# Layer B's context kept in HBM as f32 and shaped in layer B; affine parts and the variance's eps on VectorE

## What is computed

```python
x = x + tanh(g_xattn[0]) * L0_xattn(ctx, layernorm(x), mask, ...)   # 8 heads of 64
x = x + tanh(g_ffn[0])   * L0_ffn(layernorm(x), ...)                # 8 experts, top 2
x = x + tanh(g_xattn[1]) * L1_xattn(ctx, layernorm(x), mask, ...)   # 16 heads of 64
x = x + tanh(g_ffn[1])   * L1_ffn(layernorm(x), ...)                # quantised, depthwise conv
# in both attentions
ctx_n = (ctx - mean) * rsqrt(var + 1e-5) * gamma + beta             # gamma, beta per layer
lat_n = layernorm(latents) * gamma_lat + beta_lat
kv    = concat(ctx_n, lat_n)         # 375 + 112 = 487 keys
```

## Time and profile before

| what | us |
|---|---|
| median of 3 executions | 1544.24 |
| their range | 1537.44 to 1548.83 |
| profiled execution: span from its first to its last instruction | 1538.1 |
| PE, DVE, ACT, POOL busy in it | 1278.3, 1053.8, 979.1, 1107.9 |

### The profile page before, as it was taken

One profiled execution on the slowest core, in us unless ns is written; L12 is line 12 of the kernel. 1 busy time (PEld: TensorE's weight loads), 2 busy tenths in 40 slices (PEclk: granted clock), 3 DMA queues, 4 the chain that ended last, 5 costly groups with the idle time before them and its releaser, 6 DMA issues.

```text
span 1538.1 us, 45142 instructions
## 1 busy us (share of the span) xinstructions
PE 1278.3 (83%) x16918; PEld 994.2 (65%) x16918; DVE 1053.8 (69%) x2830; ACT 979.1 (64%) x2319; POOL 1107.9 (72%) x1359
## 2 busy tenths in 40 slices
PE   0778787679878989878999999899999999998852
PEld 0556565557667866656887887667676676766642
DVE  4768788977556656665666666777777777877634
ACT  2778787456455666554656566678777777777631
POOL 4768788687557755466777776788878888787653
PEclk9989999879999989989999999999999999999965
DMA  9599997486999954368999997344555444555310
GB/s 314 134 193 235 246 239 174 83 221 188 218 233 252 233 95 97 73 159 171 247 258 231 269 247 181 79 97 98 105 91 94 90 105 94 106 82 91 79 32 6
DMA packets 438329, 239.96 MB, mean 156 GB/s; under 512 B 388848, under 2 KB 420320, under 8 KB 429024
## 3 DMA queue, kind: packets, MB, share of 16 engines
q1 hardware_dynamic: 408216, 178.51, 55.7%
q10 hardware_dynamic: 26824, 51.22, 10.6%
q0 software_dynamic: 3072, 7.34, 1.6%
HBM read 107.78 MB, written 35.50 MB: 93 GB/s over the span
## 4 chain that ended last, share of the span: by engine, by line
PE 39%; ACT 13%; DVE 12%; POOL 11%; issue 9%; DMA 9%; DVEq 3%; SPq 2%; ACTq 1%; POOLq 0%
PE bank_ring L1088 9%; PE bank_ring L1126 6%; PE bank_ring L1074 5%; PE bank_out L1107 5%; DVE scores L1340 4%; DMA expert_up<-experts_up 4%; ACT scores L849 4%; PE bank_x L1187 3%; POOL probs L654 3%; PE bank_scores L1048 3%; ACT probs L856 3%; PE bank_x L1140 3%; DMA probs_turned<-probs 3%; ACT values L876 2%; DMA context<-in_ctx 2%
## 5 line engine op out<-in xcount | busy, mean ns | idle before, releaser
L654 POOL TENSOR_TENSOR probs<-scores,probs 112x487 f16<-112x487 f32 x384 | 425.0, 1123 | 234.2 <-ACT probs L856 229.1
L849 ACT ACTIVATE scores<-scores,score_min 112x487 f32<-112x487 f32 x384 | 265.8, 693 | 121.0 <-DVE score_min L1340 118.2
L1357 DVE SCALAR_TENSOR_TENSOR values<-bank_ring,values 128x512 f16<-128x512 f32 x192 | 132.4, 689 | 216.4 <-ACT values L876 216.3
L1340 DVE CUSTOM_DVE_ANT_0 scores<-bank_scores,mask 112x487 f32<-112x487 f32 x384 | 238.1, 657 | 2.9 <-PE bank_scores L1048 2.9
L856 ACT ACTIVATE probs<-scores 112x487 f16<-112x487 f32 x384 | 214.2, 604 | 24.4 <-DMA probs_turned<-probs 9.0
L1088 PE MATMUL bank_ring<-weights,kv_B 128*128 128x128 f16 x3072 | 198.3, 223 | 1.2 <-DVE keys L1352 1.2
L876 ACT ACTIVATE values<-bank_ring 128x512 f16<-128x512 f32 x192 | 112.9, 588 | 128.9 <-PE bank_out L1107 125.2
L1088 PEld LDWEIGHTS bank_ring<-weights,kv_B 128*128 128x128 f16 x3072 | 187.2, 100 | 10.5 <-DVE keys L1352 2.0
L1107 PE MATMUL bank_out<-values,probs_turned 128*128 128x64 f16 x4608 | 171.9, 195 | 17.7 <-issue 11.4
L1074 PE MATMUL bank_ring<-kv_B,weights 128*128 128x488 f16 x768 | 181.0, 372 | 0.0
L1107 PEld LDWEIGHTS bank_out<-values,probs_turned 128*128 128x128 f16 x4608 | 160.1, 100 | 21.4 <-issue 14.0
(11 more groups left out here) (230 smaller groups left out, 2470.9 us busy)
## 6 DMA issues: line engine op xcount, KB each, us to landing
expert_up<-experts_up SPq DMA_DIRECT2D x43, 1024.0 KB, 5.5
expert_down<-experts_down SPq DMA_DIRECT2D x43, 512.0 KB, 6.6
raw_weights<-in_weights ACTq DMA_DIRECT2D x8, 1536.0 KB, 10.7
experts_up<-expert_up ACTq DMA_DIRECT2D x8, 1024.0 KB, 4.4
raw_weights<-in_weights ACTq DMA_DIRECT2D x6, 1024.0 KB, 8.0
probs_turned<-probs SPq DMA_TRANSPOSE x384
context_turned_B<-kv_B ACTq DMA_DIRECT2D x16, 375.0 KB, 8.7
kv_B<-context_turned_B ACTq DMA_DIRECT2D x16, 375.0 KB, 3.7
```

The lines of the kernel that those rows point to most:

```text
L654: pool.tensor_tensor(PR[:, u % 4, 1, 0:KEYS], S[:, u % 4, 0:KEYS], PR[:, u % 4, 0, 0:KEYS], ALU.subtract).then_inc(probs_split, 1)
L849: act_e.activation(S[:, u % 4, 0:KEYS], S[:, u % 4, 0:KEYS], ACT.Exp, bias=rmin[:, u % 4:u % 4 + 1], scale=-1.0, accum_out=rsum[:, g % 2, ...
L1340: dve.tensor_tensor_reduce(out=S[:, u % 4, 0:KEYS], in0=bS[u % 2][0:TOK, 0:KEYS], in1=mask[:, m, 0:KEYS], scale=1.0, scalar=3.0e38, op0=AL ...
L1357: dve.scalar_tensor_tensor(vN[:, j % 2, 1].rearrange("p t d -> p (t d)"), bank("v", j)[:], 1 / WSCALE, vN[:, j % 2, 0].rearrange("p t d -> ...
```

## The change

The context of layer B is no longer finished in layer A. What goes to HBM is `rawT` itself (f32, normalised and turned, 128 rows of 3000 bytes a sequence) in place of hi and lo (also 3000 bytes a row, but in four pieces of 750 bytes). In layer B it comes back into `rawT`, DVE multiplies by gamma and adds beta in place (`shape_context`), ACT rounds it with one copy, POOL subtracts. For layer A, DVE writes the shaped f32 into `ctxA`, which lies in the second buffer of `kv[1]`, unused until layer B. The latents' affine parts are made by DVE straight from PSUM, four instructions in layer A and two in layer B in place of one copy. DVE adds the variance's eps, so that POOL's `rstd` is the power alone. `f_round` is folded into `f_scale` (add and subtract in one instruction). The mask's shaping is a function of its own behind `split_latents`, and waits for `ctx_lo` as well.

```diff
+def shape_step(n):
+    return start_b(n) - (6 if n == 0 else 8)
...
-        kv_dram = dram("context_turned_B", (NSEQ, 128, KB, 2, CTX), F16)
+        ctx_dram = dram("context_normed", (NSEQ, 128, KB, CTX), F32)
...
+        ctxA = kv[1][:, 1].rearrange("p k a c -> p (k a c)").bitcast(F32)[:, 0:KB * CTX]\
+            .rearrange("p (k c) -> p k c", k=KB)
...
             def rstd(stage, n, cols):
-                after(pool.tensor_tensor(r[:, 0:cols], m[:, 0:cols, 1], growth[:, 0:cols], ALU.mult))
-                after(pool.tensor_tensor(r[:, 0:cols], r[:, 0:cols], bias[:, 0:cols], ALU.add))
                 pool.tensor_tensor(r[:, 0:cols], r[:, 0:cols], minus_half[:, 0:cols], ALU.pow)\
                     .then_inc(rstd_ready[stage], 1)
...
-            def split_context(n, kb, layer):
-                pool.wait_ge(x1_drained, X1_AT[("p_turn", n, kb)])
-                after(pool.tensor_scalar(aff[:, 0:CTX], rawT[:, kb], ...))
-                pool.wait_ge(ctx_hi[layer], 2 * n + kb + 1)
-                pool.tensor_tensor(kv[layer][:, n % 2, kb, 1, TOK:KEYS], aff[:, 0:CTX], ...)
+            def split_context(layer, n):
+                src = ctxA if layer == 0 else rawT
+                pool.wait_ge(ctx_shaped[layer], KB * (n + 1))
+                pool.wait_ge(ctx_hi[layer], n + 1)
+                for kb in range(KB):
+                    last = pool.tensor_tensor(kv[layer][:, n % 2, kb, 1, TOK:KEYS], src[:, kb], ...)
+                last.then_inc(ctx_lo[layer], 1)
...
-                after(pool.tensor_scalar(h, h, ROUND, None, ALU.add))
-            def f_round(n):
-                pool.tensor_scalar(q2T[:, m], hacts[n % 2][:, m], ROUND, None, ALU.subtract)...
+                pool.tensor_scalar(q2T[:, 4 * j:4 * j + 4], h, ROUND, ROUND, ALU.add, ALU.subtract)\
+                    .then_inc(q2_ready, 1)
...
                 if (j + 4) % 4 == 0 and 0 < (j + 4) // 4 < NSEQ:
-                    split_context((j + 4) // 4, 1, 0)
+                    split_context(0, (j + 4) // 4)
+                for n in range(NSEQ):
+                    if j == shape_step(n) + 1:
+                        split_context(1, n)
...
             def spill_context(n):
-                act_e.wait_ge(ctx_lo[1], 2 * n + 2)
-                act_e.dma_start(kv_dram[n], kv[1][:, n % 2, :, :, TOK:KEYS]).then_inc(spilled[n % 2], 16)
+                act_e.wait_ge(x1_drained, X1_AT[("p_turn", n, 1)])
+                act_e.dma_start(ctx_dram[n], rawT[:]).then_inc(spilled, 16)
...
-                if (j + 2) % 4 == 0 and 0 <= (j + 2) // 4 < NSEQ:
-                    spill_context((j + 2) // 4)
+                if (j + 5) % 4 == 0 and 0 <= (j + 5) // 4 < NSEQ:
+                    spill_context((j + 5) // 4)
...
-                    if j == start_b(n) - (6 if n < 2 else 7):
+                    if j == shape_step(n) - 2:
                         reload_context(n)
...
+            def round_context(layer, n):
...
+                act_e.wait_ge(ctx_shaped[layer], KB * (n + 1))
+                act_e.activation(kv[layer][:, n % 2, :, 0, TOK:KEYS], ctxA if layer == 0 else rawT[:], ACT.Copy)\
+                    .then_inc(ctx_hi[layer], 1)
...
             def round_latents(n):
-                        last = act_e.activation(dst[:, kb, 0], latT[:, kb], ACT.Identity, scale=scale, bias=shift)
+                act_e.activation(latq[:, n % 2, :, 0], latT[:, 0], ACT.Copy)
+                act_e.activation(kv[0][:, n % 2, :, 0, 0:TOK], latT[:, 1], ACT.Copy).then_inc(lat_hi[0], 1)
...
+            def shape_context(n):
...
+                dve.wait_ge(ctx_back, 16 * (n + 1))
+                for kb in range(KB):
+                    scale, shift = latent_vec(8 + V_GAMMA, kb)
+                    dve.tensor_scalar(rawT[:, kb], rawT[:, kb], scale, shift, ALU.mult, ALU.add)\
+                        .then_inc(ctx_shaped[1], 1)
...
                 if name == "p_turn":
                     if n:
-                        dve.wait_ge(ctx_lo[0], 2 * (n - 1) + kb + 1)
-                        dve.wait_ge(ctx_lo[1], 2 * (n - 1) + kb + 1)
+                        dve.wait_ge(spilled, 16 * n)
+                        dve.wait_ge(ctx_lo[0], n)
                     dve.tensor_copy(rawT[:, kb], bX1[:, 0:CTX]).then_inc(x1_drained, 1)
+                    dve.drain()
+                    dve.tensor_scalar(ctxA[:, kb], rawT[:, kb], scale, shift, ALU.mult, ALU.add)\
+                        .then_inc(ctx_shaped[0], 1)
                 elif name in ("p_lat", "b_lat"):
-                    dve.tensor_copy(latT[:], bX1[:, 0:KB * TOK]...).then_inc(x1_drained, 1)
+                    for i, c in enumerate((8 + V_GLAT,) if layer else (V_GLAT, V_GATED)):
+                        for kb in range(KB):
+                            last = dve.tensor_scalar(latT[:, i, kb], bX1[:, TOK * kb:TOK * kb + TOK], scale, shift,
+                                                     ALU.mult, ALU.add)
```

150 lines of the change are left out of this document (60 added, 90 removed).

## The result

The changed kernel is slower: 1564.38 us median (4 runs, 1559.36 to 1570.24) against 1546.53 for the kernel before (4 runs, 1537.44 to 1549.43), a ratio of 1.0126 [1.0085, 1.0166]. The forecast was 1524.

The account below looks back on a forecast made before the run. No engine is full; waits in each engine's order of work count, PE's largest being for POOL's mask (29.5 us). Terms -10, 0, -7, -2, +1.5, +2, -4.4 sum to -20: span 1518, median 1524; 8-in-10 range 1503 to 1552.

Parts of the forecast that it names:

- Loop 62 to 263: Layer A's seven sequences beside the expert weights: POOL's and ScalarE's relief less VectorE's added work, -10 us.
- I take half: Layer A loop: of 3.0 us a sequence if all terms lay in series, 1.5 counted, times seven sequences.
- absorbed: Rival: relieved engines did not set layer A's step, VectorE fills the gap; -5 us, 1539; chance 0.22.
- 263 to 340: Routing stretch, VectorE fullest: its +5 us for two sequences is given back by work leaving POOL's queue; 0.
- 340 to 575: First expert tiles: POOL's shorter queue lets probabilities and expert loads go earlier; -7 us (0 to -16).
- The spill: Context's DMA to HBM: fewer runs, so its issue holds ScalarE less; -2 us (0 to -7).
- a late spill: Rival: spills behind 3 MB of weights land too late for VectorE's next copy; +9 on the forecast, 1533; chance 0.08.
- Prologue: Start: first spill stands behind the third context's load and the next copy follows at once; +1.5 us.
- The end: Last steps, POOL on the chain: f_round goes and two rstd are shorter; -4.4 us (-2.5 to -5).
- Layer B: PE's wait for the latents' copy grows 0.15 us each, ScalarE has 0.3 more a sequence; +2 us.
- PE covers most: Layer B: PE's work hides most of the added waits and ScalarE work, leaving +2 us.
- VectorE sets layer A: Rival: shapings held by POOL lengthen nine sequences of layer A by up to 2.6 us; +18, 1562; chance 0.13.

Follow-up runs that it names:

- b1: Kernel before with two extra POOL subtracts on idle buffers in layer B, at the step where the changed kernel splits: 1553.33 us, ratio 1.0047.
- g1: Kernel before with only the rounding constant's two additions folded into one instruction, so f_round is gone: 1553.58 us, ratio 1.011.
- f3: Kernel before with the rounding constant folded in the last two sequences only: 1551.99 us (12 runs), ratio 1.0045.
- r1: Changed kernel run once more, nothing altered: 1572.75 us (one run).
- e1: Changed kernel with layer B's context splits on POOL one step later: 1549.31 us, ratio 1.0026.
- e6: Changed kernel with VectorE's combine one step later in layer B, splits left at their step: 1550.77 us, ratio 1.0066.
- f2: Changed kernel with the fold of the rounding constant undone except in the last two sequences: 1554.69 us, ratio 1.0081.
- e3: Changed kernel with layer B's splits one step later and the latents' affine parts back on ScalarE and POOL: 1542.43 us, ratio 0.9996.
- n1: Changed kernel with layer B's splits one step later, without the context's spill and reload (output wrong): steps 58 to 106 take 398.6 us in place of 405.5.
- e2: Changed kernel with layer B's splits one step later and layer A's context affine back on ScalarE and POOL: 1570.73 us, ratio 1.0211.

## Why the prediction was wrong

Terms as the prediction put them, and what was measured. Its stretches, cut by the same clock of the program, are steps 0 to 28, 28 to 38, 38 to 60 and 60 on; "routing" in the table above begins two steps earlier than its second. For steps up to 106 the figures are the mean of the kernels that share the edit's state (before, b1, g1, f3 against changed, r1, e1, e6, f2; in 60 to 106 without e6), behind that the first profiles alone.

- *Loop 62 to 263, -10 (ends -21 and +18):* 204.0 against 208.8, +4.8. Steps -2 to 26 are equal (193.4 and 193.4), steps 26 and 27, in which the routing begins, grew from 15.8 to 21.5. The busy times moved as named beforehand, in steps -2 to 26 POOL -33% (151.0 to 100.5), ScalarE -16, VectorE +12, and the wait for the mask went. The length stayed. The step that failed is "I take half": the rows show PE's wait for the mask (20.6 to 1.9) replaced by one for VectorE's copy of the context (1.0 to 12.9) and one for turned probabilities from the DMA (3.5 to 12.0). The rival *absorbed* had this right up to step 26. Which of VectorE, the loads and the DMA transposes holds the stretch stays open.
- *263 to 340, 0 (ends +5 and -6):* 85.7 against 87.4, +1.7, inside. VectorE was the fullest engine in the whole routing, steps 26 to 38 (101.5 against 108.9, +7.4), and the latents on it, sized at 0.267 us each, took 0.387 (mean of 96; 1.16 a sequence over the copy they replace, not 0.7). e3 gives the 7.4 back, so the latents are the cause; but three sequences make 3.5 us of VectorE's time, and how the rest comes about isn't shown.
- *340 to 575, -7 (-16 to 0):* 235.8 against 223.4, -12.4. Right in kind and inside its ends.
- *The spill, -2 (0 to -7):* its issue takes 0.33 us in the median and 2.8 at most, in place of 0.92 and 4.8. The relief is there, in a loop that got no shorter. No row shows VectorE waiting for the spill: the rival *a late spill* falls.
- *Prologue, +1.5 (0 to +3):* -1.9 (46.4 to 44.5), the other way. *The end, -4.4:* 104.9 to 100.4, -4.5, right; the fold alone gives 4.2 of it (g1), though POOL saves 1.7 us a sequence by it and not 2.45.
- *Layer B, +2 (ends -5 and +8):* +6 in steps 60 to 106 and +26 in 106 to 186. This is the step that decided, "PE covers most". Its own terms were about right: the copy of 750 columns took 0.826 us (0.82 forecast), the shapings 0.46, PE's wait for the latents' copy grew from 13.7 to 16.8 (3.1; 1.5 forecast). Two things were not in it. The shorter POOL queue, which the prediction books as -2.4 us and follows no further, moved POOL's subtracts onto VectorE's combine: 11.7 us by the fold alone (g1), 26 to 33 with the splits behind. And the reload got no cost at all, only "issued two steps before its use"; n1 puts 5 to 7 us on it, in single executions.

The groups that the sum rested on, after: VectorE's latents, layer A's shaping, the apply that stood for it in the earlier trace rows, and ScalarE's copy.

```profile
L1591 DVE TENSOR_SCALAR latents_turned<-bank_x,vectors 128x112 f32<-128x112 f32 x96 | 31.8, 387 | 0.0
...
L1582 DVE TENSOR_SCALAR kv_B<-context_turned,vectors 128x375 f32<-128x375 f32 x32 | 18.3, 571 | 3.1
L1375 DVE TENSOR_SCALAR context<-context,mean_var_P,rstd_P 125x256 f32<-125x256 f32 x48 | 17.8, 426 | 1.2 <-POOL rstd_P L599 1.2
...
L909 ACT ACTIVATE kv_B<-context_turned 128x750 f16<-128x750 f32 x16 | 13.2, 826 | 0.0
```

The rival *VectorE sets layer A* named 1562, near the result by luck and with the wrong place: of the 32 shapings seven took 0.73 to 0.96 us and the others 0.47 to 0.52 (mean 0.571, 0.6 forecast), and layer A up to step 58 is not longer. What it feared, a VectorE instruction held by POOL, came in layer B. The two levels that the prediction read from L1396 are not levels: 30 of its 48 took 0.40 to 0.45 us, the other 18 anything from 0.52 to 1.06. The Trainium skill (SBUF — State Buffer, "Who interferes with whom") says that a VectorE instruction with two SBUF inputs contends with a GpSimd instruction that reads SBUF. The trace agrees for the subtracts (0.48 to 1.4 and 3.1 us) and not for `f_round`, which reads SBUF too: the 18 combines that ran under it took 0.48. The prediction drew the tensor_scalar case from that section and did not look for other VectorE instructions that POOL's moved work would meet.

Not settled: why the kernel with the context's affine part back on ScalarE and POOL (e2) is slower than the kernel before, which has more of that work; what caused the wait of 11.5 us in its profile isn't known. e2 keeps the latents and eps on VectorE and both halves of the split in one place, and these were not tried one by one there.

## What to carry to other kernels

An instruction that is taken away is also a place in time that is taken away: before one engine's queue is shortened, list what will now start earlier and which instructions of the neighbour engines it meets there, above all ones with two inputs in SBUF. A saving on an engine that isn't last is worth nothing by itself (POOL -51 us in steps -2 to 26, length unchanged), and it can cost. Of a transfer that is moved, ask what else lands in its new steps, not only how long its issue takes.

## What the runs showed of the hardware that was not expected

- A two-input VectorE instruction of 0.48 us took up to 3.1 us beside an unbroken row of POOL subtracts of 0.9 to 1.3 us each: its delay of 2.6 us is longer than two of them, so it was held over several instructions and not for one. Of the 71 combines held in plain layer B of the changed kernel (both profiles), e1 and g1, 70 ended 0.27 to 0.29 us after the end of a subtract. It goes the other way too: in e6, where eight combines start 0.09 us ahead of a subtract, they take 0.48 and the subtract 1.37 in place of 1.1.
- Under a POOL instruction with one input (2.45 us, 128x896) the same instruction took 0.48 in all 18 places of the kernel before, and in the 18 each of b1 and f2. That the one input is the reason isn't shown: no other such instruction met a combine.
- Behind five of the six pairs held for 3.1 us the granted clock was at the 1.2 GHz level for 3.4 us, which cost 1.3 us on one group of 24 matmuls, and the step took 10.35 to 10.83 us. Behind the sixth PE waited as long (2.92 us), the clock stayed at 2.4 GHz, and the step took 8.82. In g1, where this wait is at most 1.8 us, the clock fell behind none of the nine pairs.
